# Transposes of a set in one block ahead of the gathers, in a two-layer spectral and deformable convolution kernel

## The reference, cut to what matters

```python
def _L1_conv_ref(x, w_om, b_om, weight, bias):
    om = lax.conv_general_dilated(x, w_om, ...) + b_om[None, :, None, None]
    off = om[:, :2 * K2].reshape(-1, K2, 2, Ho, Wo)
    mask = jax.nn.sigmoid(om[:, 2 * K2:])
    ...
    vals = jax.vmap(_bilinear_sample)(x, ys, xs)
    vals = vals * mask[:, None]
    out = jnp.einsum('bckhw,ock->bohw', vals, weight.reshape(Oc, -1, K2))
    return out + bias[None, :, None, None]

x = x + _L0_conv_ref(_gn(x), ...)
x = x + _L1_conv_ref(_gn(x), ...)
```

## Time and profile before

| what | us |
|---|---|
| median of 3 runs | 1808.21 (1806.97 to 1809.94) |
| the profiled execution | 1805.23 |
| span of its instructions | 1803.3 |
| PE busy | 1703.3 (94%) |
| DVE / ACT / POOL busy | 1329.7 / 1174.5 / 891.7 |
| mean granted TensorE clock | 0.969 |

### The profile page before, as it was taken

How to read it: one execution, slowest core, us unless ns; L and a number is a source line. 1 busy time by engine, 2 the same in 40 slices (tenths; PEclk the granted TensorE clock), 3 DMA queues, 4 the chain that set the end, 5 groups by cost and what they waited for, 6 DMA issues and landing times.

```text
span 1803.3 us, 159696 instructions
## 1 busy us (share of the span) xinstructions
PE 1703.3 (94%) x70913; PEld 1319.3 (73%) x70913; DVE 1329.7 (74%) x2056; ACT 1174.5 (65%) x1971; POOL 891.7 (49%) x1153
## 2 busy tenths in 40 slices
PE   8886479999999999999999999999999999999985
PEld 3521257888888888888888888888888888888874
DVE  7387457777777777777777777777777777777762
ACT  7148246667767667777667677667677677676652
POOL 0000245556555556555556555555555565555550
PEclk9799599999999999999999999999999999999997
DMA  9148632333333333333333233333333333333320
GB/s 385 26 186 364 228 120 74 98 97 87 88 93 97 97 96 87 88 95 97 97 95 89 81 94 97 97 93 87 89 96 97 97 89 88 93 96 97 97 57 13
DMA packets 161679, 195.95 MB, mean 109 GB/s; under 512 B 20288, under 2 KB 136672, under 8 KB 157536
## 3 DMA queue, kind: packets, MB, share of 16 engines
q1 hardware_dynamic: 161632, 195.34, 36.6%
HBM read 143.05 MB, written 52.22 MB: 108 GB/s over the span
## 4 chain that ended last, share of the span: by engine, by line
PE 90%; DMA 3%; DVE 2%; issue 2%; ACT 1%; POOL 0%; DVEq 0%; SPq 0%; POOLq 0%; ACTq 0%
PE pE L1076 18%; PE pVV L1156 16%; PE pE L1097 13%; PE pM L1122 10%; PE pVV L1097 8%; PE pR L1110 7%; PE pVV L1110 7%; PE pM L1132 4%; PE pE L991 3%; DMA xh_scratch<-stg 2%; PE pE L1048 1%; DMA win<-xh_scratch 1%; DVE big L799 1%; ACT stg L592 1%; PE pVV L1026 0%
## 5 line engine op out<-in xcount | busy, mean ns | idle before, releaser
L523 POOL COPY big<-win 128x480 f32<-128x480 f32 x520 | 290.6, 588 | 654.5 <-PE pVV L1110 438.3
L511 POOL TENSOR_TENSOR prod<-big 128x600 f32<-128x600 f32 (+1 forms) x489 | 498.5, 1040 | 29.6 <-POOL big L546 29.5
L633 ACT ACTIVATE big<-pE 128x768 f32<-128x768 f32 x390 | 334.8, 858 | 186.8 <-PE pE L1076 186.8
L832 DVE COPY big<-pE 128x768 f32<-128x768 f32 x390 | 372.9, 956 | 100.1 <-PE pE L1076 87.5
L838 DVE STREAM_TRANSPOSE big<-prod 128x768 f32<-128x768 f32 x390 | 377.4, 968 | 15.8 <-POOL prod L511 15.8
L1076 PE MATMUL pE<-big,sel_s 32*64 32x192 f32 x12480 | 358.8, 338 | 12.5 <-DVE big L832 10.3
L1076 PEld LDWEIGHTS pE<-big,sel_s 32*64 32x64 f32 x12480 | 220.2, 132 | 115.7 <-issue 64.0
L1156 PE MATMUL pVV<-big,wc 64*32 64x128 f32 x18720 | 295.7, 273 | 4.3 <-issue 3.3
L1156 PEld LDWEIGHTS pVV<-big,wc 64*32 64x32 f32 x18720 | 263.2, 106 | 46.5 <-issue 46.3
L1097 PE MATMUL pE<-big 60*32 60x72 f32 x20800 | 251.4, 232 | 17.1 <-issue 17.1
L1097 PEld LDWEIGHTS pE<-big 60*32 60x32 f32 x20800 | 230.2, 105 | 24.2 <-issue 18.9
(11 more groups left out here) (97 smaller groups left out, 1675.7 us busy)
## 6 DMA issues: line engine op xcount, KB each, us to landing
big<-xh_scratch SPq DMA_DIRECT2D x390, 136.0 KB
win<-xh_scratch SPq DMA_DIRECT2D x130, 408.0 KB, 3.7
xh_scratch<-stg SPq DMA_DIRECT2D x32, 544.0 KB, 3.4
big<-in_x SPq DMA_DIRECT2D x16, 1024.0 KB, 15.7
x_scratch<-big SPq DMA_DIRECT2D x16, 1024.0 KB, 4.4
x1r<-x_scratch SPq DMA_DIRECT2D x256, 64.0 KB, 3.0
out<-outs SPq DMA_DIRECT2D x256, 64.0 KB, 2.1
xh_scratch<-zero SPq DMA_DIRECT2D x4, 204.0 KB, 2.6
```

What stands on the lines that cost most here:

```text
L511: made = nc.gpsimd.tensor_tensor(prod[:, kx, at:at + m, 0:SQ].rearrange("p m (a b) -> p m a b", a=NSH), hy.to_broadcast(shape), hx.to_broa ...
L523: last = nc.gpsimd.tensor_copy(strips[:, half * HTP:(half + 1) * HTP, h, 0:REG].rearrange("p t (r x) -> p t r x", r=WIN_R), tiles_of(q, h, ...
L633: nc.scalar.activation(*expanded(kx, 0), ACT.Copy).then_inc(e_read, 1)
L832: nc.vector.tensor_copy(*expanded(kx, 1)).then_inc(e_read, 1)
```

## The change

On PE all transposes of set N now stand in step N: turn_rows(N, 0), (N, 1), (N, 2), then turn_offsets(N+3), then turn_rows(N, 3), then the gathers. Nothing stands between the last gather and the branch. ACT's copies follow the same order. The first two gather groups now write pE, the last writes pVV; the transposes use pR, pV[0], pV[1], pR. spread(N, 0), which writes pE, therefore waits only for the second group's copies (`n * NG - 1`). Each gather group has a wait of its own on xt_done. On POOL both `cut_tiles` stand last in the step, behind the products. convolve loses its wait on xt_done.

```diff
-        pG = [pV, [pE[:, 0:512], pE[:, 512:1024]], [pE[:, 1024:1536], pE[:, 1536:2048]]]
-        pT = [pR, pV[0], pV[0], pR]
+        pG = [[pE[:, 0:512], pE[:, 512:1024]], [pE[:, 1024:1536], pE[:, 1536:2048]], pV]
+        pT = [pR, pV[0], pV[1], pR]
...
             def step(N, s, on, place):
                 if on[1]:
-                    cut_tiles(N + 1, 1 - s % 2, 0)
                     product(N + 1, (s + 1) % RING, 1)
                     product(N + 1, (s + 1) % RING, 2)
...
                 if on[1]:
+                    cut_tiles(N + 1, 1 - s % 2, 0)
                     cut_tiles(N + 1, 1 - s % 2, 1)
...
                 if on[0]:
                     table(N, 2)
-                    turned(N, 2)
-                    turned(N, 3)
+                    for k in range(TCH):
+                        turned(N, k)
...
-                if on[1]:
-                    turned(N + 1, 0)
-                    turned(N + 1, 1)
...
                 if kx == 0:
-                    wait(pe, v_act, n * NG)
-                    wait(pe, v_dve, n * NG)
+                    wait(pe, v_act, n * NG - 1)
+                    wait(pe, v_dve, n * NG - 1)
...
                 if gi == 0:
-                    wait(pe, conv_read, n)
                     pe.wait_ge(e_read, (n * ROUNDS + ROUNDS) * 2)
-                    pe.wait_ge(xt_done, n * TCH + 3)
-                    pe.nop(nofuse=True)
-                if gi == 1:
-                    pe.wait_ge(xt_done, n * TCH + TCH)
-                    pe.nop(nofuse=True)
+                pe.wait_ge(xt_done, n * TCH + 2 + gi)
+                pe.nop(nofuse=True)
...
-                wait(pe, xt_done, min((n + 1) * TCH + 2, SETS * TCH) if isinstance(n, int) else n * TCH + (TCH + 2))
...
                 if on[0]:
                     spread(N, 2)
-                    turn_rows(N, 2)
-                    turn_rows(N, 3)
+                    for k in range(TCH - 1):
+                        turn_rows(N, k)
                 if on[3]:
                     turn_offsets(N + 3)
                 if on[0]:
+                    turn_rows(N, TCH - 1)
                     for gi in range(NG):
                         gather(N, gi)
-                if on[1]:
-                    turn_rows(N + 1, 0)
-                    turn_rows(N + 1, 1)
```

More of the change, by code:

```diff
@@ L1101, in turn_rows @@
             def turn_rows(n, k):
-                wait(pe, xt_done, n * TCH + k - k % 2)
-                pe.wait_ge(strips_done, n * 2 + (k // 2 + 1))
+                if k == 0:
+                    wait(pe, xt_done, n * TCH)
                 if k == 1:
-                    wait(pe, v_act, (n - 1) * NG + 1)
-                if k == 2:
                     wait(pe, conv_read, n)
+                if k == 3:
+                    pe.wait_ge(xt_done, n * TCH + 1)
+                if k % 2 == 0:
+                    pe.wait_ge(strips_done, n * 2 + (k // 2 + 1))
                 for u in range(TPC):
```

## The result

The changed kernel takes 1846.93 us (median of four runs, 1846.25 to 1850.12), the kernel before on the same chip 1807.59 us. The ratio is 1.022, interval 1.0202 to 1.0237: **slower by 39 us**. The forecast was 1819 us, the range ended at 1835. The direction was right, the size was not: 11 us were forecast.

A forecast was written before the change was run, and what follows sets the result against it. PE's time line was taken as the bound. +0.16 us a step times 125 gave +20, front -8, end -1: +11 us on the profiled 1805.2, 1816; the median stands 3 us higher, so 1819 us, range 1801 to 1835.

The forecast's parts named there:

- What bounds the kernel: Middle stage: only PE's own time line counts, with PE busy 94% of the span; other engines matter where PE waits.
- The transposes taken forward: PE's step start: transposes taken forward and put in front of the gathers, +0.82 us a step.
- The new wait: Ahead of the third gather group: an added register operation with a wait, priced 0.10 us, +0.09 us a step.
- Behind the last gather: Loop end: spread(N+1,0) starts 0.48 us after the last gather's start, behind the bare branch; 1.18 becomes 0.48, -0.70 us.
- convolve's wait: Between spread 0 and convolve: the wait for ACT's copy goes, 0.90 becomes 0.83 us, -0.06 us a step.
- The step in sum: First transpose to next convolve: 6.63 us against 6.47, +0.16 us a step, times 125 +20 us.
- Front and end: Before and after the steady steps: products ahead of POOL's cuts give -8 us; a shorter gather stall at the end, -1.
- The branch is hidden after all: Rival, loop end: PE's queue covers the branch, spread 0.2 us after the last gather, -0.12 a step, 1784 us; chance 0.18.
- The wait behind the loop head as late as today: Rival, loop head: 0.6 us instead of 0.48 before spread, +0.28 us a step, 1834 us; chance 0.10.
- The copies become the bound: Rival: DVE's copy of gather 1 adds time only if over 0.5 us late; said to decide nothing, no chance given.

The follow-up runs named there:

- after_one_wait_less: Changed kernel, but the second gather group waits for all four turned blocks and the third waits for nothing; 1826.32 us, 1.0113 of the kernel before.
- after_both: Changed kernel with the loop's branch moved behind offsets(N+3) and the third gather group's wait removed; 1781.12 us, 0.9862 of the kernel before.
- after_branch_moved: Changed kernel, same order of work, PE's loop cut so that the branch stands behind offsets(N+3); 1800.81 us, 0.9973 of the kernel before.
- after_no_register_op: Changed kernel with both copied-gather counters started at 1, so spread(N,0) needs no register operation behind the loop head; 1835.61 us, 1.0173 of the kernel before.
- before_cuts_last: Kernel before with only POOL's order changed, both cuts last in the step; 1797.87 us, ratio 0.9957.
- before_branch_long: The control: kernel before, same order of work, PE's loop branch moved behind offsets(N+3); 1807.34 us, ratio 1.0011.

## Why the prediction was wrong in size, point by point

- **What bounds the kernel.** Right: PE's time line. But the steps that failed are both in it: what follows the last gather, and the third wait. The first is idle time in the page's sense; the second hardly shows there, as 17.6 us of it stood in the busy row.
- **The transposes taken forward.** Right: turn_offsets starts 1.36 us after the first transpose (forecast 1.37), the fourth block 1.95 (1.95), gather 0 2.52 (2.48).
- **The new wait.** Right in kind, wrong in size: forecast +0.09, measured 0.16 by the branch rows of after_one_wait_less, 0.15 by those of after_both against after_branch_moved. I priced the gap alone, from one place; the gap is as forecast (0.11), and some 0.05 a step more come with the wait. Where they arise stays open. In the step shown, gather 2 starts at 4.60 (4.50).
- **Behind the last gather.** This is the term that failed most. Forecast: spread 0.48 us after the last gather; measured 0.58 to 0.62. The sequencer's records follow the forecast to the tenth: register operation 1012.3, branch 0.1 later, loop head 0.3 after that. Then the forecast has the wait 0.1 behind the loop head, and there stands a register operation first (1012.8), the wait at 1012.9. I had read the loop head of the kernel before and costed the new one by it, while the diff turns `n * NG` into `n * NG - 1`; PE's instruction list of the changed kernel shows the operation. after_no_register_op takes it out and has 0.49.
- **convolve's wait.** Right: 0.84 us behind spread 0 instead of 0.90.
- **The step in sum.** convolve comes 1013.84 - 1006.94 = 6.90 us after the first transpose, against 6.63 forecast and 6.47 before. Of the missing 0.27, gather 0's start has 0.04, from there to gather 2 0.06, inside and around the third group 0.04, the bare branch 0.13. Each is small; 124 steps make 33 us of them. The means over 400 to 1700 us say the same: the gathers grew by 0.19 us where about 0.09 was forecast, the stretch from the last gather to spread 0 shrank by 0.58 instead of 0.70, and the gathers start 0.04 later than forecast. That is 0.26 of the 0.28 us a step between +0.16 and +0.44.
- **Front and end.** Forecast -8 and -1; first and last branch give -10.3 and -2.5, POOL's order alone -7.8 in all. Good to 4 us, and before_cuts_last shows POOL's order to be the cause of the larger part. The stall of 0.65 us at the first gather of the last steps is gone wholly, where I had left half. In the changed kernel that place reads:

```profile
1790.54 0.65 PE L1105 MATMUL pR<-ident,big 128*128 128x128 f32 x4
1791.12 1.76 PE L1090 MATMUL pE<-big 60*32 60x72 f32 x130
```

- **The rivals.** "The branch is hidden after all" (0.18) is refuted three times: the bare branch costs 0.39 us a step in the changed kernel and 0.33 in the kernel before, and the control shows that it was covered. The rival's price was off as well: it had 1784 and -0.12 us a step with the branch hidden and the wait in place, and after_branch_moved, which is that case, has 1800.81 and +0.05. after_both comes to 1781, but only with the wait taken out too. The Trainium skill (Advanced Engine Details and Errata, Engine Queue Depths) has a depth of 64 for TensorE, "complicated with tiling"; in these tiled gathers the queue did not cover the branch, which cost 0.39 us a step. The Trainium skill (Advanced Engine Details and Errata, Control Flow Timing) has about 108 ns for a compare-and-branch, the median here is 208. "The wait behind the loop head as late as today" (1834) gave nearly the measured gap, 0.6, but for another reason: it blamed DVE's copy, and it was the register operation. "The copies become the bound" never showed.
- **The range.** It took the bounds of one term at a time, and the wait had none. The branch stood at its upper end and the wait past its price at once, and a term that repeats 124 times carries an error of 0.1 us into 12 us. With the branch at 0.6 and the wait at its measured price together, the sum would have been about 1843 (0.16 + 0.12 + 0.07 is 0.35 a step, +43 us, less 9 for the ends).

## What to carry to other kernels

Where matmuls start 0.02 us apart, the sequencer was only 0.1 us ahead of the array here, and a branch, a register operation or a wait behind or between them showed in the time. Where they start further apart (transposes, 0.11 us each, or the offsets, 12 in 1.1 us) it had got ahead, and the same branch cost nothing. That the short spacing is the reason is a reading of these traces; no run changed the spacing alone. So put a hardware loop's branch behind matmuls that the sequencer gets ahead of, and look for that before a block is moved that happens to stand at the loop's end. One order of work can be cut at any point, and the cut is free to choose: here it was worth 46 us with the order untouched. When a step of a loop is costed from the old trace, read the new program's instructions at its head and around each wait as well, since a value that is off by one can cost a register operation in every round. And a busy share that stays the same doesn't show that the work took as long as before: where records overlap, short pauses between their starts count as busy.

## What the runs showed of the hardware

- A compare-and-branch of PE takes 208 ns in the median (76 ns the shortest record); those of the other engines' loops in the kernel before take 45 ns (ACT, POOL, SP) and 56 ns (DVE) in the median. Register operation, branch and loop head together keep PE's array idle for 0.33 to 0.39 us a round behind tiled fp32 matmuls that start 0.02 us apart, and nothing behind the offsets' matmuls, where the sequencer was 0.9 us ahead when the branch came, or behind two blocks of transposes (before_branch_long: step 11.78 in both places).
- A register operation at the loop head, in the open, costs about 0.1 us a round (a gap of 0.58 to 0.62 us for 0.49).
- A register operation with a wait that is satisfied long before costs 0.11 us as a gap inside such gathers, and 0.15 to 0.16 us a round in sum.
- From the gathers' last start to a spread, another shape of tile, pass 0.22 us with a register operation and a satisfied wait between them, but no branch; transposes of one shape start 0.11 us apart.
- The stretch from the first gather to the third group is 0.1 us longer in some steps of the changed kernel than in others. The cause was not found. It isn't POOL's second cut, and without the third wait the steps still differ as much (all gathers 2.75 to 2.91 us, 2.89 to 3.06 with it).
